# Two output products moved, eight scaled tiles given to ScalarE, and one softmax spread, in a state-space scan kernel

## The chip, the cores and the metric

The kernel runs on one core of a Trainium2 chip. The time is the device time of one launch in microseconds; the median of several runs is compared. Five engines work side by side, each through its own list of instructions in order, and hand work to each other with semaphores: TensorE (PE; its weight loads are listed as PEld), VectorE (DVE), ScalarE (ACT), GpSimd (POOL) and SyncE (SP), which issues the transfers.

## The reference, cut to what matters

One block on x of shape (2, 1024, 256): a row gate, a Mamba layer, then an attention and a gated network on its output. What the change touches is the Mamba recurrence and its projection, and the attention's scores:

```python
def step(h, inputs):
    d_t, x_t, B_t, C_t = inputs
    dA = jnp.exp(d_t[..., None] * A)
    h = dA * h + (d_t * x_t)[..., None] * B_t[:, None, :]
    y = jnp.einsum('bds,bs->bd', h, C_t)      # 16 states are summed
    return (h, y)
...
y = ys.transpose(1, 0, 2) + xi * D
y = y * jax.nn.silu(z)
return x + y @ out_proj                        # the output product
...
scores = jnp.einsum('bhte,bhse->bhts', qmod, k) / jnp.sqrt(jnp.asarray(e, x.dtype))
attn = jax.nn.softmax(scores, axis=-1)
```

There are 512 channels, 16 states to a channel, 1024 positions in each of two batches. All is computed in float32.

## The kernel before, in words

The positions are cut into four chunks of 512 (two to a batch). A chunk passes 16 states; a counter n from 0 to 63 runs over chunk and state, c = n // 16 and s = n % 16. For every n the work is:

- ACT makes four exponentials dA (L1259, one to each 128 channels), DVE runs four scans over the 512 positions (L1727), and POOL has written the scans' other input into a ring of four tiles beforehand (L1403).
- PE turns the four position tiles of the scanned state (`transposes`, L834) into the two banks of `hT`: tiles 0 and 2 into bank 0, tiles 1 and 3 into bank 1. They are turned in the order 1, 0, 3, 2. Tile 3 waits until tile 1 has been read from its bank, tile 2 until tile 0 has.
- Tiles 0 and 2 are scaled by C on ACT (L1269, `mul_step`) and added up by PE in `yacc` (`reduce`, L597, with the skip products of L593 in a chunk's first state). Tiles 1 and 3 are scaled and added into `yTd` by DVE (`mac_step`): L1747 for s > 0, and L1740 for s = 0, which starts the sum without adding. For some states tile 3 is scaled by ACT (L1278) and added by POOL (L1415).

Everything else is cut into jobs, each one product group of PE in one of two banks `pp` that take turns in the jobs' order (`INDEX`), and its reader or readers on ACT or DVE. Tables place them by hand in half states: a chunk has 32, two to a state, the even one being served before exp_step(n, 2) on ACT and before scan_step(n, 2) on DVE. A job at half state h is issued by PE in h, and read by ACT and DVE in h + 1. In an even half PE issues `transposes(n - 1, 1)` first, then the jobs, then tiles 0, 3 and 2. A job waits until the job two before it has been read. The tables are `PROLOGUE` (the next chunk's input: T the transposed input, I and Z the input products, V the convolutions, X, XT and D the products for B, C and delta), `EPILOGUE` (the chunk before: Y the last sums times the gate, O the output products at L626 with their sum into `xt` at L1553, R their transposes), `LAST_EPILOGUE` for the same in the last chunk, and `ATT` (batch 0's attention, beside the last chunk). D's reader is long: ACT takes |x| from the bank (L1108), then an exponential and a logarithm (L1128, L1130), then DVE adds them (L1538) and frees the bank. S0 and S1 are the two halves of the scores (L698). S1's reader is the softmax: DVE adds and reduces (L1572 to L1580), ACT takes one exponential of 1024 columns (L1158), and DVE waits for it.

After state 63 a tail of 68 us follows: the last chunk's epilogue, batch 1's attention and the gated network.

## Time and profile before

| | |
|---|---|
| median of 3 runs | 565.59 us (562.24 to 568.28) |
| the profiled execution's own time | 562.97 us |
| its span in the profile | 561.2 us |
| first scan starts, last scan ends | 44.5 us, 493.5 us |
| busy PE, DVE, ACT, POOL | 481.0, 461.2, 372.5, 387.2 us |

The span is shorter than the device time by what lies around it. The busy times are sums over stages with different limits; a row of the timeline gives an instruction's start, its duration, its engine, line and operation, and in brackets how long the engine idled before it and what released it. Instructions of the same form that follow each other are merged in one row (x2, x4). One float32 product is recorded as two instructions, so 16 PE rows are 8 products.

### The profile page before, as it was taken

How to read it: one execution, taken by the hardware profiler on the slowest of the kernel's cores; microseconds unless marked ns; L12 is line 12 of the kernel's file. 1: busy time of each engine (PE TensorE's matmuls, PEld its weight loads, DVE VectorE, ACT ScalarE, POOL GpSimd, SP SyncE). 2: the span in 40 equal slices, each digit the busy share in tenths (PEclk: the TensorE clock that was granted, in tenths of full speed). 3: DMA queues.
4: the chain of work that ended last, by engine and by line, in shares of the span. 5: the costliest groups of instructions: out<-in, count | busy, mean ns of one | idle time of the engine just before them, and what ended most of it. 6: DMA issues, size and time to landing. Idle time of an engine off the chain costs nothing.

```text
span 561.2 us, 7944 instructions
## 1 busy us (share of the span) xinstructions
PE 481.0 (86%) x2777; PEld 348.8 (62%) x2777; DVE 461.2 (82%) x531; ACT 372.5 (66%) x650; POOL 387.2 (69%) x235
## 2 busy tenths in 40 slices
PE   8968999868768999987689999986897968899992
PEld 6423765455557665745576657656796856888651
DVE  4779989979999889799997897899998989851522
ACT  3676777769966767898757678897568668721210
POOL 5039978767996877879968778599789969510001
PEclk9987999979989999899899999598998869799997
DMA  8330111111111001111010111111111590029004
GB/s 289 115 116 38 39 38 39 40 40 37 39 37 39 38 39 39 40 39 39 39 39 37 39 37 41 38 38 38 39 39 39 201 369 1 2 87 353 2 1 155
DMA packets 17919, 38.88 MB, mean 69 GB/s; under 512 B 1665, under 2 KB 10497, under 8 KB 17874
## 3 DMA queue, kind: packets, MB, share of 16 engines
q1 hardware_dynamic: 17874, 38.32, 19.8%
q8 instruction: 24, 0.39, 0.3%
q14 instruction: 21, 0.17, 0.1%
HBM read 36.08 MB, written 2.23 MB: 68 GB/s over the span
## 4 chain that ended last, share of the span: by engine, by line
PE 49%; DVE 27%; issue 11%; ACT 10%; POOL 2%; DVEq 0%; ACTq 0%; POOLq 0%
DVE scanmem L1727 16%; PE hT L834 11%; PE pp L563 6%; PE pp L539 6%; PE yacc L597 5%; DVE yTd L1747 5%; PE pp L626 4%; ACT dA L1259 2%; PE dA L799 2%; PE pp L575 2%; PE pp L589 2%; ACT hc L1269 1%; PE pp L770 1%; PE pp L649 1%; DVE yTd L1652 1%
## 5 line engine op out<-in xcount | busy, mean ns | idle before, releaser
L1403 POOL TENSOR_TENSOR scanmem<-par,scanmem 128x1024 f32<-128x1024 f32 x128 | 300.9, 2370 | 79.7 <-PE hT L834 60.3
L834 PE MATMUL hT<-con,scanmem 128*128 128x128 f32 x1024 | 167.4, 298 | 54.0 <-DVE yTd L1747 32.0
L1259 ACT ACTIVATE dA<-par,Aneg 128x512 f32<-128x512 f32 x256 | 171.7, 690 | 56.0 <-DVE scanmem L1727 54.5
L834 PEld LDWEIGHTS hT<-con,scanmem 128*128 128x128 f32 x1024 | 126.7, 152 | 108.2 <-issue 34.3
L1727 DVE TENSOR_TENSOR_SCAN scanmem<-dA,carry,scanmem 128x512 f32<-128x512 f32 x128 | 156.7, 1266 | 11.9 <-ACT dA L1259 11.7
L1727 DVE TENSOR_TENSOR_SCAN scanmem<-dA,scanmem 128x512 f32<-128x512 f32 x128 | 148.9, 1204 | 8.5 <-ACT dA L1259 7.8
L1269 ACT ACTIVATE hc<-hT,CTs 128x512 f32<-128x512 f32 x128 | 87.1, 680 | 43.5 <-PE hT L834 43.3
L597 PE MATMUL yacc<-con,hc 128*128 128x128 f32 x512 | 86.6, 297 | 0.3 <-ACT hc L1269 0.3
L597 PEld LDWEIGHTS yacc<-con,hc 128*128 128x128 f32 x512 | 69.4, 157 | 0.6 <-ACT hc L1269 0.6
L1747 DVE SCALAR_TENSOR_TENSOR yTd<-hT,CTs,yTd 128x512 f32<-128x512 f32 x85 | 62.0, 729 | 8.4 <-PE hT L834 7.5
L539 PE MATMUL pp<-xnT,wi 128*128 128x512 f32 x120 | 59.0, 620 | 3.4 <-ACT xnT L1038 2.1
L563 PE MATMUL pp<-xr,diag 128*128 128x512 f32 x112 | 50.2, 592 | 0.0
L1463 POOL TENSOR_TENSOR par<-xt,hc 128x1024 f32<-128x1024 f32 x1 | 2.4, 2350 | 53.0 <-ACT hc L1319 53.0
L539 PEld LDWEIGHTS pp<-xnT,wi 128*128 128x128 f32 x120 | 21.6, 198 | 22.2 <-issue 17.4
L563 PEld LDWEIGHTS pp<-xr,diag 128*128 128x128 f32 x112 | 20.3, 189 | 21.1 <-issue 20.9
L626 PE MATMUL pp<-wo,par 128*128 128x256 f32 x128 | 29.0, 381 | 0.5 <-DVE par L1507 0.5
L1415 POOL TENSOR_TENSOR yTd<-yTd,sm 128x512 f32<-128x512 f32 x21 | 26.9, 1280 | 0.0
L626 PEld LDWEIGHTS pp<-wo,par 128*128 128x128 f32 x128 | 23.8, 190 | 3.9 <-DVE par L1507 0.7
L1415 POOL TENSOR_TENSOR yTd<-yTd,xnT 128x512 f32<-128x512 f32 x14 | 17.8, 1274 | 8.1 <-ACT xnT L1278 8.1
L589 PE MATMUL pp<-dbc,wdt 17*128 17x512 f32 x28 | 17.3, 706 | 0.4 <-DVE xt L1553 0.3
L1538 DVE SCALAR_TENSOR_TENSOR par<-pp,par 128x512 f32<-128x512 f32 x14 | 9.6, 688 | 9.3 <-ACT par L1130 6.4
L799 PE MATMUL dA<-con 128*128 128x128 f32 x110 | 17.1, 289 | 0.0
(195 smaller groups left out, 510.8 us busy)
## 6 DMA issues: line engine op xcount, KB each, us to landing
scanmem<-brow SPq DMA_DIRECT2D x32, 512.0 KB, 3.6
par<-in SPq DMA_DIRECT2D x1, 4096.0 KB, 17.3
scanmem<-in SPq DMA_DIRECT2D x1, 4096.0 KB, 15.0
xt<-in SPq DMA_DIRECT2D x4, 512.0 KB, 6.7
wi<-in SPq DMA_DIRECT2D x2, 1024.0 KB, 6.7
out<-par SPq DMA_DIRECT2D x4, 512.0 KB, 4.1
aw<-in SPq DMA_DIRECT2D x5, 256.0 KB, 6.7
xr<-in SPq DMA_DIRECT2D x1, 1024.0 KB, 8.9
```

The source lines that it names most:

```text
L539: last = mm(o, win[:, k, col:col + P], xnT[:, k, :], start=k == 0, stop=k == KD - 1)
L563: last = mm(o, dg[:, m, k, :], xr3[:, m, k:k + T], start=k == 0, stop=k == KC - 1)
L589: return mm(o, wdt[:, m * P:(m + 1) * P], dbc[0:DR + 1, :], start=True, stop=True)
L597: return mm(o[:, m * P:(m + 1) * P], src, ident, start=False, stop=last, is_transpose=True, skip_group_check=True)
L626: last = mm(o[:, i * DM:(i + 1) * DM], dx(e)[:, m, t0:t0 + P], wo[:, m, :], start=m == 0, stop=m == CT - 1)
L834: last = nc.tensor.transpose(hT[:, i % 2, m * P:(m + 1) * P], hb[:, n % RING, m, i * P:(i + 1) * P], ident)
L1259: A(dA[:, m % 2, :], delta(c)[:, m, :], ACT.Exp, scale=Aneg[:, m * NS + s:m * NS + s + 1]).then_inc(da_ready, 1)
L1269: A(hc[:, e % 2, :], hT[:, 0, :], ACT.Copy, scale=CTs[:, c % 2, i, s:s + 1]).then_inc(mul_done, 1)
L1403: nc.gpsimd.tensor_tensor(hb[:, n % RING, ms, :], dx(c)[:, ms, :], Bb[:, row:row + 1, :].to_broadcast([P, 2, T]), ALU.mult).then_inc(bx_re ...
L1415: nc.gpsimd.tensor_tensor(dst, dst, for_pool(n), ALU.add).then_inc(pool_sum_done, 1)
L1727: V.tensor_tensor_scan(hb[:, n % RING, m, :], dA[:, m % 2, :], hb[:, n % RING, m, :], start, ALU.mult, ALU.add).then_inc(scan_done, 1)
L1747: V.scalar_tensor_tensor(dst, src, cs, dst, ALU.mult, ALU.add).then_inc(mac_done, 1)
```

## The change

1. In `EPILOGUE`, for chunks 0 and 1 (read beside chunks 1 and 2), output product ("O", 0) stands at half state 18 instead of 11 and ("O", 1) at 20 instead of 18.
2. The first state's tiles 1 and 3 of every chunk are written into `yTd` by ACT (`first_sum`) instead of by DVE: eight instructions of 128x512. A semaphore of their own, `first_sum_done`, replaces `mac_done` for those states, and `wait_sum` chooses between them. On ACT they stand in state 1 of the chunk: tile 1 after mul_step and carry_step, ahead of the jobs and of exp_step(n, 2); tile 3 after mul_step(n - 1, 0).
3. In `ATT`, S1 moves from half state 17 to 18, PT from 20 to 21, YV, YT and VV from 22, 23, 24 to 23, 24, 25, and WO from 27 to 28.

```diff
-EPILOGUE = {1: [("Y", 1), ("Y", 3)], 11: [("O", 0)], 18: [("O", 1)], 28: [("R", 0)], 30: [("R", 1)]}
+EPILOGUE = {1: [("Y", 1), ("Y", 3)], 18: [("O", 0)], 20: [("O", 1)], 28: [("R", 0)], 30: [("R", 1)]}
-ATT = [7, 8, 8, 10, 12, 14, 15, 16, 17, 20, 22, 23, 24, 27]
+ATT = [7, 8, 8, 10, 12, 14, 15, 16, 18, 21, 23, 24, 25, 28]
...
+def scalar_sums(n, i):
+
+    return 2 * (n // NS) + (i + 1) // 2
...
+        def wait_sum(eng, n, i):
+
+            if n % NS == 0:
+                eng.wait_ge(first_sum_done, scalar_sums(n, i))
+            elif i == 3 and by_pool(n):
+                eng.wait_ge(pool_sum_done, pool_sums(n))
+            else:
+                eng.wait_ge(mac_done, vector_sums(n, i))
...
+            def first_sum(n, i):
+
+                c = n // NS
+                act.wait_ge(hT_ready, turned(n, i))
+                if c >= 2 and i == 1:
+                    wait_full(act, ("Y", c - 2, 3))
+                A(yTd[:, c % 2, i // 2, :], hT[:, 1, :], ACT.Copy, scale=CTs[:, c % 2, i, 0:1]).then_inc(first_sum_done, 1)
...
+                    if s == 1:
+                        first_sum(n - 1, 1)
                     for job in to_read(2 * n):
                         read(job)
                     exp_step(n, 2)
...
                     if n:
                         mul_step(n - 1, 0)
                         pool_mul_step(n - 1)
+                    if s == 1:
+                        first_sum(n - 1, 3)
...
-                if i == 3 and by_pool(n):
+                if s == 0 or i == 3 and by_pool(n):
                     return
                 dve.wait_ge(hT_ready, turned(n, i))
                 dst = yTd[:, c % 2, i // 2, :]
                 src, cs = hT[:, 1, :], CTs[:, c % 2, i, s:s + 1]
-                if s == 0:
-                    if c >= 2 and i == 1:
-                        wait_full(dve, ("Y", c - 2, 3))
-                    V.tensor_scalar(dst, src, cs, None, ALU.mult).then_inc(mac_done, 1)
...
+                wait_sum(dve, n - 1, i)
+                V.scalar_tensor_tensor(dst, src, cs, dst, ALU.mult, ALU.add).then_inc(mac_done, 1)
```

How PE's list changes around half states 10 to 12 of chunk 1 (L563 is V, L626 is O; the transposes and sums are L834 and L597). Before:

```order
L563 MATMUL pp<-xr,diag 128x512 x4
L834 MATMUL hT<-con,scanmem 128x128 x8
L597 MATMUL yacc<-con,hc 128x128 x4
L834 MATMUL hT<-con,scanmem 128x128 x4
L597 MATMUL yacc<-con,hc 128x128 x4
L626 MATMUL pp<-wo,par 128x256 x8
L834 MATMUL hT<-con,scanmem 128x128 x4
L563 MATMUL pp<-xr,diag 128x512 x4
L834 MATMUL hT<-con,scanmem 128x128 x8
```

Now (all lines are 15 further down in the new file):

```order
L578 MATMUL pp<-xr,diag 128x512 x4
L849 MATMUL hT<-con,scanmem 128x128 x8
L612 MATMUL yacc<-con,hc 128x128 x4
L849 MATMUL hT<-con,scanmem 128x128 x4
L612 MATMUL yacc<-con,hc 128x128 x4
L849 MATMUL hT<-con,scanmem 128x128 x4
L578 MATMUL pp<-xr,diag 128x512 x4
L849 MATMUL hT<-con,scanmem 128x128 x8
```

The eight products O are gone from between one state's last sum and the next state's first transposes, and V follows those at once.

PE's list at half states 18 to 21 of chunk 1 (L598 is XT, L604 is D, L641 is O), in the new file:

```order
L641 MATMUL pp<-wo,par 128x256 x8
L849 MATMUL hT<-con,scanmem 128x128 x8
L612 MATMUL yacc<-con,hc 128x128 x4
L849 MATMUL hT<-con,scanmem 128x128 x4
L612 MATMUL yacc<-con,hc 128x128 x4
L598 MATMUL pp<-con,dbc 128x49 x4
L604 MATMUL pp<-dbc,wdt 128x512
L849 MATMUL hT<-con,scanmem 128x128 x4
L641 MATMUL pp<-wo,par 128x256 x8
L604 MATMUL pp<-dbc,wdt 128x512
L849 MATMUL hT<-con,scanmem 128x128 x8
```

Before, the same rows stood here without the second L641: the second D followed four transposes directly. Now O's eight products stand between them, and ahead of the transposes of tiles 0 and 3.

ACT's list in states 16 to 18, where chunk 1 begins (L1274 exponentials, L1284 the scaled tiles for PE, L1301 the new first sums, L1053 T's reader), in the new file:

```order
L1274 ACTIVATE dA<-par,Aneg 128x512 x2
L1284 ACTIVATE hc<-hT,CTs 128x512
L1301 ACTIVATE yTd<-hT,CTs 128x512
L1274 ACTIVATE dA<-par,Aneg 128x512 x2
L1284 ACTIVATE hc<-hT,CTs 128x512
L1301 ACTIVATE yTd<-hT,CTs 128x512
L1274 ACTIVATE dA<-par,Aneg 128x512 x2
L1284 ACTIVATE hc<-hT,CTs 128x512
L1053 ACTIVATE xnT<-pp,vec 128x512 x2
```

Before, the two L1301 were absent. The first now stands ahead of state 17's last two exponentials and of the scaling of tile 0.

## Rows read from the trace of the kernel before

**Rows 1.** The page: span, and the chain that ended last.

```profile
span 561.2 us, 7944 instructions
...
PE 49%; DVE 27%; issue 11%; ACT 10%; POOL 2%; DVEq 0%; ACTq 0%; POOLq 0%
```

**Rows 2.** Groups by line: busy us, mean ns, idle before, releasers.

```profile
L1740 DVE TENSOR_SCALAR yTd<-hT,CTs 128x512 f32<-128x512 f32 x8 | 5.8, 729 | 0.3 <-PE hT L834 0.2
```

**Rows 3.** Timeline, states 20 to 23: start, us, engine, line, operation.

```profile
202.65 3.62 PE L626 MATMUL pp<-wo,par 128*128 128x256 f32 x16
...
203.06 0.72 DVE L1747 SCALAR_TENSOR_TENSOR yTd<-hT,CTs,yTd 128x512 f32<-128x512 f32 x1
...
206.10 0.60 PE L834 MATMUL hT<-con,scanmem 128*128 128x128 f32 x4
...
206.54 3.60 PE L563 MATMUL pp<-xr,diag 128*128 128x512 f32 x8
...
210.62 0.69 ACT L1269 ACTIVATE hc<-hT,CTs 128x512 f32<-128x512 f32 x1 [3.74 <-PE hT L834]
...
213.15 2.45 DVE L1727 TENSOR_TENSOR_SCAN scanmem<-dA,carry,scanmem 128x512 f32<-128x512 f32 x2
```

**Rows 4.** Timeline of states 37 and 38, same place in chunk 2.

```profile
315.29 0.72 DVE L1747 SCALAR_TENSOR_TENSOR yTd<-hT,CTs,yTd 128x512 f32<-128x512 f32 x1
...
318.95 0.60 PE L834 MATMUL hT<-con,scanmem 128*128 128x128 f32 x4
```

**Rows 5.** Timeline of states 25 and 26, chunk 1.

```profile
234.57 1.12 PE L589 MATMUL pp<-dbc,wdt 17*128 17x512 f32 x2
...
235.63 1.95 PE L834 MATMUL hT<-con,scanmem 128*128 128x128 f32 x8
...
237.41 0.69 DVE L1538 SCALAR_TENSOR_TENSOR par<-pp,par 128x512 f32<-128x512 f32 x1 [1.51 <-ACT par L1130]
...
238.43 0.67 ACT L1269 ACTIVATE hc<-hT,CTs 128x512 f32<-128x512 f32 x1
```

**Rows 6.** Windows: us, busy (instructions) of PE, PEld, DVE, ACT, POOL, PEclk, DMA.

```profile
241.00:245.00 4.00, 2.75 (x13) 1.37 (x13) 4.00 (x6) 3.94 (x7) 3.57 (x2) 1.00 0.00 0
...
352.00:356.00 4.00, 4.00 (x12) 2.17 (x12) 3.97 (x5) 3.61 (x7) 3.29 (x2) 0.50 0.00 0
```

**Rows 7.** Timeline of states 17 and 18, where chunk 1 begins.

```profile
169.28 0.69 ACT L1259 ACTIVATE dA<-par,Aneg 128x512 f32<-128x512 f32 x1 [1.84 <-DVE scanmem L1727]
...
170.56 0.75 DVE L1740 TENSOR_SCALAR yTd<-hT,CTs 128x512 f32<-128x512 f32 x1
171.08 0.67 ACT L1269 ACTIVATE hc<-hT,CTs 128x512 f32<-128x512 f32 x1
...
172.30 0.60 PE L834 MATMUL hT<-con,scanmem 128*128 128x128 f32 x4
...
174.06 1.95 PE L533 MATMUL pp<-par,xt 128*128 128x128 f32 x16
...
176.10 1.26 ACT L1038 ACTIVATE xnT<-pp,vec 128x512 f32<-128x512 f32 x2
```

**Rows 8.** Timeline of states 49 and 50, where chunk 3 begins.

```profile
397.73 0.66 PE L834 MATMUL hT<-con,scanmem 128*128 128x128 f32 x4 [1.11 <-DVE yTd L1740]
...
402.02 3.69 PE L626 MATMUL pp<-wo,par 128*128 128x256 f32 x16
402.40 2.45 DVE L1727 TENSOR_TENSOR_SCAN scanmem<-dA,carry,scanmem 128x512 f32<-128x512 f32 x2
```

**Rows 9.** Timeline of states 56 and 57: batch 0's S1, R and softmax.

```profile
448.78 0.60 ACT L1141 ACTIVATE x1T<-pp 128x512 f32<-128x512 f32 x1 [1.02 <-PE pp L698]
...
449.86 0.68 DVE L1572 TENSOR_TENSOR sm<-pp,negm 128x512 f32<-128x512 f32 x1
...
452.68 1.15 ACT L1158 ACTIVATE sm<-sm,st 128x1024 f32<-128x1024 f32 x1 [3.29 <-DVE st L1580]
...
454.53 4.83 DVE L1727 TENSOR_TENSOR_SCAN scanmem<-dA,carry,scanmem 128x512 f32<-128x512 f32 x4 [0.41 <-ACT dA L1259]
```

More of the change, by code:

```diff
@@ L163, in pool_sums @@
     return sum(by_pool(j) for j in range(n + 1))
+def scalar_sums(n, i):
+    return 2 * (n // NS) + (i + 1) // 2
 def vector_sums(n, i):
-    return 2 * n + (i + 1) // 2 - pool_sums(n if i == 3 else n - 1)
+    return 2 * n + (i + 1) // 2 - pool_sums(n if i == 3 else n - 1) - 2 * (n // NS + 1)
 def to_read(h):
@@ L346, in build @@
         pool_mul_done, pool_sum_done = sem("pool_mul_done"), sem("pool_sum_done")
+        first_sum_done = sem("first_sum_done")
         carry_done, gated = sem("carry_done"), sem("gated")
@@ L826, in transposes @@
                 if i == 3:
-                    pe.wait_ge(mac_done, vector_sums(n, 1))
+                    wait_sum(pe, n, 1)
                 if i == 1 and n:
@@ L831, in transposes @@
                     else:
-                        pe.wait_ge(mac_done, vector_sums(n - 1, 3))
+                        wait_sum(pe, n - 1, 3)
                 for m in range(CT):
@@ L1408, in add_step @@
                 if by_pool(n):
-                    if by_pool(n - 1):
-                        pool.wait_ge(pool_sum_done, pool_sums(n - 1))
-                    else:
-                        pool.wait_ge(mac_done, vector_sums(n - 1, 3))
+                    wait_sum(pool, n - 1, 3)
                     pool.wait_ge(pool_mul_done, pool_sums(n))
@@ L1736, in mac_step @@
                 src, cs = hT[:, 1, :], CTs[:, c % 2, i, s:s + 1]
-                if s == 0:
-                    if c >= 2 and i == 1:
-                        wait_full(dve, ("Y", c - 2, 3))
-                    V.tensor_scalar(dst, src, cs, None, ALU.mult).then_inc(mac_done, 1)
-                else:
-                    if i == 3 and by_pool(n - 1):
-                        dve.wait_ge(pool_sum_done, pool_sums(n - 1))
-                    else:
-                        dve.wait_ge(mac_done, vector_sums(n - 1, i))
-                    V.scalar_tensor_tensor(dst, src, cs, dst, ALU.mult, ALU.add).then_inc(mac_done, 1)
+                wait_sum(dve, n - 1, i)
+                V.scalar_tensor_tensor(dst, src, cs, dst, ALU.mult, ALU.add).then_inc(mac_done, 1)
             for c in range(NCH):
```

## The prediction

> **What bounds the kernel now.** I read the page first, then the groups by line, then the timeline in those places that the change touches, and the windows for TensorE's clock. The page's chain of waits goes through PE for 49% and DVE for 27% of a span of 561.2 us [rows 1]: neither engine alone sets the pace, and a saving on one of them counts only in those states in which the chain runs through it. The tail behind the last scan is not touched. So the sum is made state by state: for each place, which wait ends last before the next state's first scan, and by how much that moves.
>
> **Part 1a, O leaves half state 11: a gain.** In chunk 1, ("O", 0) starts at 202.65 and takes 3.62 us [rows 3]. Behind it in PE's list stand state 21's transposes of tile 1 at 206.10 and then V at 206.54. What these transposes need is a sum of DVE that begins at 203.06 and takes 0.72, so they could have begun at 203.85. V's 3.60 us then stand ahead of the transposes of tile 0, for which ACT waits 3.74 us until 210.62, and behind ACT's copy stand V's two readers, two exponentials, and the scans of state 23 at 213.15 [rows 3]. The whole chain from 206.10 to 213.15 hangs on PE, so it moves forward by 206.10 - 203.85 = 2.25 us. The next candidate is DVE itself: it loses O's two sums between the scans of state 22 and gets tile 1 earlier, so it is through before V's reader can run, and does not cut the gain. In chunk 2 the same sum of DVE begins at 315.29, and the transposes stand at 318.95 instead of about 316.1 [rows 4]: 2.85 us. Together **-5.1 us**. Nothing of O's work has vanished; it stands elsewhere.
>
> **Part 1b, an O at half state 18.** There ("O", 1) stood, now ("O", 0) stands: eight products and two sums of DVE for the same. Zero.
>
> **Part 1c, O enters half state 20: a loss.** The second product D starts at 234.57, and the next transposes at 235.63 [rows 5]. Now O stands ahead of D: from about 234.5, 3.62 us [rows 3] to 238.1. D itself must now wait for the first D's bank, since O took the turn between them; DVE reads that bank from 237.41 for 0.69, to 238.10 [rows 5], just covered by O. D starts at 238.2, the transposes of tile 0 at 238.2 + 1.06 = 239.25, done at about 239.85. ACT took them at 238.43 [rows 5]. ACT is the bound here, with the table load, softplus and exponentials; so 3.6 us of O meet 2.2 us of room, and its list moves back by 239.85 - 238.43 = 1.4 us. Behind that copy are the second D's readers and state 27's exponentials, all of which move with it. O's two sums on DVE fit in DVE's wait for the second softplus. Twice (chunks 1 and 2): **+2.8 us**, if PE keeps its full clock.
>
> It may not. PE took 1.95 us for eight transposes at 235.63 [rows 5] where four follow each other in 0.44 at full clock (206.10 to 206.54 [rows 3]), so about 1.1 for eight: the low level, 1.2 GHz, had just set in after the light work of XT and D. The price has these ends. If all of O runs at the low level in both chunks, it takes 3.6 us more each time, +7.2. Or the denser work of O ends the low stretch sooner: in chunk 2, at 352 to 356, PE shows a granted clock of 0.50 and is busy 4.00 us for 12 instructions, where the like stretch of chunk 1, at 241 to 245, shows 1.00 and 2.75 us for 13 [rows 6]; taking that away is worth up to 1.25 us there. I take zero between them: one effect offsets the other, and the rows are nearest to a stretch that begins at full clock. "TensorE: Matmul & The Clock Gate" in the Trainium skill, Part 1 (the warmup mystery), says that the clock gate gives full rate to a busy array and half rate after idling. By that rule O is good for the clock once it runs, but starts behind light work; the sum would be anywhere between the two ends.
>
> **Part 2, the first sums go to ACT.** Eight instructions of 0.729 us leave DVE, 5.8 us in all [rows 2], and eight enter ACT's list. Copies of this shape take ACT 0.67 [rows 7]. What counts is what is queued behind them. In chunk 1 the exponential of state 17 ran at 169.28, while tile 1 was ready to be read only just before 170.56 [rows 7]. Now ACT waits for tile 1, copies it from 170.4 on, and does both exponentials behind it, so that the scaling of tile 0 moves from 171.08 to 172.4. DVE, freed of two instructions, would reach state 18 1.1 us sooner. But the transposes of tile 2 need that scaled tile's bank: PE, which came there at 172.30 [rows 7], starts at 173.1, and T moves from 174.06 to 174.9 and ends at 176.8. Its last copy ends at 177.5, where it ended before at 176.10 + 1.26 = 177.4 [rows 7]. The input products and the exponentials of state 19 hang on that copy. DVE's gain is gone two states later: 0 in chunk 1, and the same order gives 0 in chunk 2. In chunk 0 the copy stands ahead of Z's two readers on ACT and delays them and T by some 0.3 to 0.6 us, against 0.85 us that DVE gains: 0 again. Each of these zeros could be 0.5 off either way.
>
> Chunk 3 has no T behind it. There PE's transposes of tile 3 wait 1.11 us for DVE's first sum until 397.73 [rows 8]; ACT can now copy tile 1 before its exponentials are due. DVE drops two instructions, about 1.3 us with their overlap; ACT's second copy gives 0.2 of it back ahead of state 50's exponential. The last gate, O at 402.02 and state 50's scans at 402.40 [rows 8] come 1.1 us sooner. Nothing there restores the old time: **-1.1 us**.
>
> **Part 3, S1 one half state later.** PE now issues S1 after state 56's transposes of tile 1, so 0.44 us later (the step of four in [rows 3]). R's reader on ACT must wait for S1, since it overwrites what S1 reads: it ran at 448.78, after a wait of 1.02 [rows 9], and now runs at 449.2, and state 57's last two exponentials follow it. DVE's second pair of scans starts at 450.4 instead of 454.53 [rows 9], but the softmax now stands behind them: from 449.86 (DVE) by 452.68 (ACT) to 454.53 (next scans) it took 4.7 us [rows 9], and it takes them again, since state 58's exponentials are queued behind the softmax's exponential. State 58 would start at 457.5; it started at 454.53 + 2.4 = 456.9 [rows 9]. In exchange, the copies for PE and POOL are made ahead of the stall instead of behind it, and state 58 loses its own wait: about 0.9 us back. Together **-0.3 us**; ends are -1.5 and +2, the latter if nothing is given back and R waits longer. PT to WO one half state later are small products in states with room: zero.
>
> **Sum:** -5.1 + 2.8 - 1.1 - 0.3 = **-3.7 us**. The profiled execution took 562.97 us, which gives 559.3. The median of the runs is 565.59, 2.6 us above that execution, so the number that I give is 565.6 - 3.7 = **561.9 us**. The runs of before lie within 6 us of each other, and about 1% (5.7 us) is what can be told from no change.
>
> **Rivals.** *DVE is the bound (chance 0.27).* Then the first sums' gain of 1.1 us is kept in all four chunks: three times 1.1 = 3.3 us more, -7.0, 558.6; with the clock's 1.25 of chunk 2, 557.4. For it: DVE shows no idle time ahead of its first sum in state 17 [rows 7], and T's copy ends only 0.1 us late by my walk. Against: state 19 is released by ACT and PE. "Perfetto Trace Analysis" in the Trainium skill, section Optimizing Scalar/DVE Operations, says that offloading from a saturated DVE to Scalar may make sense; by that rule the 5.8 us would count in full, a sum of -8.4. No row has DVE saturated over the whole stage.
>
> *O at half state 20 runs at the low clock (0.15); the one that ends slower.* PE's activity before it is XT, D and four transposes, and behind these it had fallen to half rate at 235.6 [rows 5]. With all of O low in both chunks, +7.2: the sum is +3.5, 569.1 us. It turns from a gain to a loss once the two O lose more than 3.7 us together, that is when more than half of them runs at 1.2 GHz.
>
> *The softmax round trip gets worse (0.16).* R's reader waits for S1, and DVE's stall is paid in full with nothing given back: +2 in place of -0.3, -1.4, 564.2.
>
> *Nothing much done:* the order shows that the instructions do move, so this is no case of its own.
>
> My forecast has the remaining 0.42. Its own range, with 0.5 for each zero and the runs' spread, is 558.5 to 565. For 8 in 10 the range must take in the DVE case and the softmax case and most of the run-to-run spread: **555.5 to 567.5**. Faster by over 1% (under 559.9): 0.24 from the DVE case and 0.11 from the lower part of mine, 0.35. Slower by over 1% (above 571.2): a third of the low-clock case and a bad draw of runs, 0.10. Within 1%: 0.55.
>
> **What would show it.** State 22, which ended at 213.15 and read ("O", 0) before, should be 2 us shorter, and its V should start within 1 us of the end of DVE's sum; so in chunk 2. State 26 should be 1.4 us longer, with ACT waiting on PE for tile 0 behind O and D. State 17 should be about 1 us shorter and states 18 and 19 take it back; chunk 3's state 49 should be shorter for good. The softmax should stand after state 57's fourth scan, with DVE still idle until ACT is through. Wrong would be: O's 16 instructions taking over 5 us, gaps on ACT in state 17 that reach the scans, or state 19 starting earlier by the full 1.1 us.

## The result: slower by half a per cent

| | before | after |
|---|---|---|
| median beside each other, 20 runs each | 562.44 us | 564.09 us |
| lowest and highest run | 558.79, 568.57 us | 561.0, 568.74 us |
| profiled execution's own time | 562.97 us | 566.36 us |
| span in the profile | 561.2 us | 564.6 us |
| mean granted clock of TensorE in it | 0.929 | 0.923 |

The ratio of after to before is 1.0054, with a 95% interval of 1.0028 to 1.0080: 3.0 us slower (1.6 to 4.5), where the prediction had 3.7 us faster. The ratio leaves out a kernel's runs that are over 1.5% above its fastest, which are five of the kernel before at 568 us and none of the new one, so the two medians over all runs are only 1.7 us apart, and the size of the rise is less sure than the interval says. Its 561.9 us were set against a first median of 565.59; beside the 20 runs the same sum gives 558.7. The rise is inside "within 1%", which had the largest chance, but the sign is wrong, and the reasons for the sign are what follows.

The page of the kernel after, beside [rows 1]; parts left out:

```profile
span 564.6 us, 7944 instructions
...
PE 51%; DVE 25%; issue 10%; ACT 9%; POOL 3%; DVEq 0%; ACTq 0%; POOLq 0%
```

DVE's share of the chain fell by 2 points, PE's rose by 2 and POOL's by 1. The L1740 group of [rows 2] is gone; eight rows of ACT, L1301, do its work. A time per state shows where the sum came apart. A state's length runs from the start of its first scan to that of the next state's; the table has those that changed by over 0.8 us.

| states | after - before, us | predicted |
|---|---|---|
| 22 and 38 (O left half state 11) | -2.3, -2.8 | -2.25, -2.85 |
| 26 and 42 (O came into 20) | +1.5, +1.5 | +1.4, +1.4 |
| 43 | -1.5 | up to -1.25, left out of the sum |
| 1, 2 (first sums, chunk 0) | -1.0, +2.7 | sum zero |
| 18 (chunk 1) | +1.4 | sum zero |
| 32, 33, 34 (chunk 2) | -0.9, -1.6, +1.1 | sum zero |
| 49 (chunk 3) | -1.3 | -1.1 |
| 57, 58 (softmax) | +3.7, -1.3 | +0.6, -0.9 |
| 11, 44, 55, 59 | +0.9, +0.9, -1.2, +1.0 | nothing |

States 10 to 12 together are 1.9 longer, though no instruction of them was moved; the kernel with part 3 alone has the like there.

One profiled execution stands here against one, and much of what the table shows comes and goes without any edit. State 43 is 8.8 us long before; it is 7.3 us in e3, e5, e7 and e16 too, which leave the outputs where they were. State 55 is 1.2 us shorter in every other profile of this case. State 58 is 6.9 us before and 5.6 us after; it is 5.5 to 5.7 us in e9, e10, e13 and e15 too, which leave S1 where it was. The tail behind the last scan, where nothing was edited, takes 67.7 us before, 69.2 us after, and 72.3 us in e10, with a granted clock of 0.94, 0.94 and 0.87. So a difference is put down to an edit below only where it comes with the edit in the other profiles too.

**Part 1 came out as worked out.** Timeline of PE and ACT in states 21 and 22, after, which answers to [rows 3]; columns are start, us, engine, line, operation, and in brackets idle time and releaser:

```profile
209.07 0.63 PE L849 MATMUL hT<-con,scanmem 128*128 128x128 f32 x4 [0.75 <-DVE yTd L1762]
209.54 3.60 PE L578 MATMUL pp<-xr,diag 128*128 128x512 f32 x8
...
213.62 0.69 ACT L1284 ACTIVATE hc<-hT,CTs 128x512 f32<-128x512 f32 x1 [1.43 <-PE hT L849]
```

PE now waits for DVE's sum, 0.75 us, and V follows the transposes at once. ACT waits 1.43 us for V's end, not 3.74. Timeline of PE in state 26, after, beside [rows 5]:

```profile
237.48 3.62 PE L641 MATMUL pp<-wo,par 128*128 128x256 f32 x16
241.15 1.12 PE L604 MATMUL pp<-dbc,wdt 17*128 17x512 f32 x2
242.20 1.09 PE L849 MATMUL hT<-con,scanmem 128*128 128x128 f32 x8
```

O runs at the full clock (3.62 us, as in [rows 3]), so the rival in which it runs at the low one is out. All seven other profiles that have O in half state 20 show states 22, 26, 38 and 42 changed by the same amounts, within 0.2 us.

**Part 3 did not.** DVE and POOL in state 57, after, beside [rows 9]:

```profile
451.01 0.69 DVE L1600 TENSOR_REDUCE st<-sm 128x1 f32<-128x512 f32 x1
451.74 4.69 DVE L1602 TENSOR_TENSOR st<-st 128x1 f32<-128x1 f32 x1
456.46 0.15 DVE L1604 TENSOR_SCALAR st<-st 128x1 f32<-128x1 f32 x1
...
458.50 2.46 DVE L1751 TENSOR_TENSOR_SCAN scanmem<-dA,carry,scanmem 128x512 f32<-128x512 f32 x2 [0.41 <-ACT dA L1274]
```

```profile
448.23 4.66 POOL L1430 TENSOR_TENSOR scanmem<-par,scanmem 128x1024 f32<-128x1024 f32 x2
452.85 1.25 POOL L1439 TENSOR_TENSOR yTd<-yTd,xnT 128x512 f32<-128x512 f32 x1
454.07 2.33 POOL L1430 TENSOR_TENSOR scanmem<-par,scanmem 128x1024 f32<-128x1024 f32 x1
```

The larger of two numbers per partition takes DVE 4.69 us. It ends at 456.43, and POOL, which had no gap since 448.23, ends its last instruction at 456.40. The same instruction in the kernel before, a row that the prediction did not read, with POOL beside it, whose last instruction ended at 452.44:

```profile
451.29 1.16 DVE L1578 TENSOR_TENSOR st<-st 128x1 f32<-128x1 f32 x1
```

```profile
450.09 2.35 POOL L1403 TENSOR_TENSOR scanmem<-par,scanmem 128x1024 f32<-128x1024 f32 x1
```

**Nor did part 2 in chunk 0.** ACT and PE in states 0 and 1, after:

```profile
54.34 0.69 ACT L1301 ACTIVATE yTd<-hT,CTs 128x512 f32<-128x512 f32 x1 [3.22 <-PE hT L849]
54.92 1.07 ACT L1117 ACTIVATE par<-pp 128x512 f32<-128x512 f32 x2
55.87 1.31 ACT L1274 ACTIVATE dA<-par,Aneg 128x512 f32<-128x512 f32 x2
57.10 0.69 ACT L1284 ACTIVATE hc<-hT,CTs 128x512 f32<-128x512 f32 x1
```

```profile
57.84 1.11 PE L849 MATMUL hT<-con,scanmem 128*128 128x128 f32 x4 [2.12 <-ACT hc L1284]
58.75 1.91 PE L608 MATMUL yacc<-par,diagD 128*128 128x128 f32 x8
```

The same stretch before:

```profile
52.36 0.60 ACT L1102 ACTIVATE par<-pp 128x512 f32<-128x512 f32 x1 [1.06 <-PE pp L539]
54.07 0.60 ACT L1102 ACTIVATE par<-pp 128x512 f32<-128x512 f32 x1 [1.12 <-PE pp L539]
54.57 0.69 ACT L1259 ACTIVATE dA<-par,Aneg 128x512 f32<-128x512 f32 x1
...
56.26 0.67 ACT L1269 ACTIVATE hc<-hT,CTs 128x512 f32<-128x512 f32 x1
```

ACT idles 3.22 us at the first sum. Two readers of Z's bank and two exponentials, which ran at 52.36 to 56.3 before, stand behind it. PE then idles 2.12 us for tile 0. When it starts again its products take 1.91 us, where eight of this form take 1.06 at full clock: the low level, 1.2 GHz (the granted clock is 0.50 from 58 to 61 us). States 0 to 4 are together 1.9 us longer.

Chunks 1 and 2 show no loss of this kind. State 18 is 1.4 us longer in five of the six profiles that have both sums of chunk 1 on ACT (2.6 in e13), but state 17 is up to 1.6 us shorter; the five states from 16 on are together between 1.3 us shorter and 1.1 us longer, and without these sums they are between 1.0 us shorter and 0.9 us longer. In chunk 2 the spread is as wide: 1.3 shorter to 1.7 longer with the sums, 1.1 shorter to 1.3 longer without.

### The profile page after: what moved, and what is told of

It reads as the page before. It is cut to its first block, busy times and chain, and to the rows that moved or that the text cites. A ratio compares the mean times of both kernels' runs of the same rounds, so it can differ in the third digit from the quotient of the medians.

```text
span 564.6 us, 7944 instructions
## 1 busy us (share of the span) xinstructions
PE 482.8 (86%) x2777; PEld 347.8 (62%) x2777; DVE 460.1 (81%) x523; ACT 376.6 (67%) x658; POOL 386.6 (68%) x235
## 4 chain that ended last, share of the span: by engine, by line
PE 51%; DVE 25%; issue 10%; ACT 9%; POOL 3%; DVEq 0%; ACTq 0%; POOLq 0%
DVE scanmem L1751 14%; PE hT L849 12%; PE pp L578 6%; PE pp L554 6%; PE yacc L612 5%; DVE yTd L1762 4%; PE pp L641 3%; PE pp L604 2%; PE dA L814 2%; POOL scanmem L1430 2%; ACT dA L1274 2%; PE pp L590 2%; PE pp L713 1%; PE yacc L608 1%; PE pp L664 1%
## 5 line engine op out<-in xcount | busy, mean ns | idle before, releaser
L849 PE MATMUL hT<-con,scanmem 128*128 128x128 f32 x1024 | 164.8, 295 | 56.9 <-DVE yTd L1762 33.0
L1274 ACT ACTIVATE dA<-par,Aneg 128x512 f32<-128x512 f32 x256 | 171.3, 690 | 40.2 <-DVE scanmem L1751 38.7
L849 PEld LDWEIGHTS hT<-con,scanmem 128*128 128x128 f32 x1024 | 124.2, 151 | 112.1 <-issue 34.1
L1284 ACT ACTIVATE hc<-hT,CTs 128x512 f32<-128x512 f32 x128 | 87.0, 680 | 42.7 <-PE hT L849 42.6
L612 PEld LDWEIGHTS yacc<-con,hc 128*128 128x128 f32 x512 | 67.9, 155 | 0.6 <-ACT hc L1284 0.6
L554 PE MATMUL pp<-xnT,wi 128*128 128x512 f32 x120 | 60.4, 632 | 2.3 <-DVE par L1554 1.4
L641 PE MATMUL pp<-wo,par 128*128 128x256 f32 x128 | 29.0, 381 | 0.5 <-DVE par L1531 0.5
L641 PEld LDWEIGHTS pp<-wo,par 128*128 128x128 f32 x128 | 23.8, 190 | 3.8 <-DVE par L1531 0.7
L604 PE MATMUL pp<-dbc,wdt 17*128 17x512 f32 x28 | 17.3, 706 | 0.9 <-DVE xt L1577 0.7
```

What stands on the lines that cost most here:

```text
L554: last = mm(o, win[:, k, col:col + P], xnT[:, k, :], start=k == 0, stop=k == KD - 1)
L612: return mm(o[:, m * P:(m + 1) * P], src, ident, start=False, stop=last, is_transpose=True, skip_group_check=True)
L641: last = mm(o[:, i * DM:(i + 1) * DM], dx(e)[:, m, t0:t0 + P], wo[:, m, :], start=m == 0, stop=m == CT - 1)
L849: last = nc.tensor.transpose(hT[:, i % 2, m * P:(m + 1) * P], hb[:, n % RING, m, i * P:(i + 1) * P], ident)
L1274: A(dA[:, m % 2, :], delta(c)[:, m, :], ACT.Exp, scale=Aneg[:, m * NS + s:m * NS + s + 1]).then_inc(da_ready, 1)
L1284: A(hc[:, e % 2, :], hT[:, 0, :], ACT.Copy, scale=CTs[:, c % 2, i, s:s + 1]).then_inc(mul_done, 1)
```

## The experiments

All ratios are to the kernel before, run beside on the same chip, with 95% intervals; two experiments may have run on different chips. A ratio is not the quotient of the two medians: for e10 the medians give 1.005 and for e12 0.990, where the ratios are 1.0011 and 0.9863. Lengths of states are from one profiled execution each, against that of the kernel before. The expectations of e13, e15, e16 and e17 speak of eight chunks and that of e14 of the last chunk of each batch; the kernel has four chunks, with two first sums each, and e14 has those of chunk 3 alone.

### One part at a time

**e1: the outputs alone** (part 1).

```diff
-EPILOGUE = {1: [("Y", 1), ("Y", 3)], 11: [("O", 0)], 18: [("O", 1)], 28: [("R", 0)], 30: [("R", 1)]}
+EPILOGUE = {1: [("Y", 1), ("Y", 3)], 18: [("O", 0)], 20: [("O", 1)], 28: [("R", 0)], 30: [("R", 1)]}
```

> The kernel before with only the two output products moved (half states 18 and 20 instead of 11 and 18). Theory (the output move is a gain, the loss is elsewhere): states 22 and 38 shorter by 2.3 and 2.8 us, states 26 and 42 longer by 1.5 each, so -2 us, or -3.5 if state 43 keeps its full clock; ratio to the kernel before 0.994 to 0.997. Rival (the output move itself loses, because the products now stand in front of the softplus readers): ratio above 1.000, with states 26 and 42 longer by 3 us or more each.

Measured 559.18 us, ratio 0.9955 (0.9924 to 0.9986), 2.5 us faster; the sum had 2.3. States 22 -2.1, 26 +1.5, 38 -2.7, 42 +1.5.

**e2: the first sums alone** (the change without its `EPILOGUE` and `ATT`).

> The kernel before with only the eight first sums given to ScalarE. Theory (ScalarE's list holds the scaled tile 0 and so T back; light work makes TensorE fall to 1.2 GHz there): chunk 0 slower by 1.5 us or more over states 1 to 3, chunk 1 slower by 0 to 1.5 over states 17 to 19, chunk 2 0 to -2, chunk 3 -1.3; ratio 0.999 to 1.004. Rival (VectorE is the bound, its 5.8 us are saved): ratio 0.990 to 0.994, states 1, 17, 33 and 49 shorter by 1.1 with nothing given back.

Measured 566.0 us, ratio 1.0080 (1.0042 to 1.0118): 4.5 us slower, where the sum had 1.1 faster. State 49 is 1.3 shorter, as worked out; states 1 and 2 together are 1.5 longer. The mean granted clock over its runs is 0.913, against 0.928 over those of the kernel before beside it. The expectation (0.999 to 1.004) missed the size as well.

**e3: the scores apart alone.**

```diff
-ATT = [7, 8, 8, 10, 12, 14, 15, 16, 17, 20, 22, 23, 24, 27]
+ATT = [7, 8, 8, 10, 12, 14, 15, 16, 18, 21, 23, 24, 25, 28]
```

> The kernel before with only the attention table of the change (S1 one half state later, PT to WO too). Theory (the softmax's maximum of 128x1, a VectorE instruction with both operands in SBUF, waits until GpSimd pauses, and now meets three of its instructions in a row): that instruction takes over 3 us instead of 1.16, state 57 is longer by 3 us or more, ratio 1.003 to 1.007. Rival (it is only the copy that waits for S1 and the exponentials behind the softmax, as I forecast): the maximum stays near 1.2 us, states 57 to 59 together within 1 us of before, ratio 0.998 to 1.002.

Measured 562.75 us, ratio 1.0036 (1.0010 to 1.0063): 2.0 us slower, state 57 longer by 3.5, 58 shorter by 1.3. DVE in state 57, and POOL beside it:

```profile
455.21 4.51 DVE L1578 TENSOR_TENSOR st<-st 128x1 f32<-128x1 f32 x1
```

```profile
451.52 4.67 POOL L1403 TENSOR_TENSOR scanmem<-par,scanmem 128x1024 f32<-128x1024 f32 x2
456.13 1.28 POOL L1415 TENSOR_TENSOR yTd<-yTd,xnT 128x512 f32<-128x512 f32 x1
457.35 2.35 POOL L1403 TENSOR_TENSOR scanmem<-par,scanmem 128x1024 f32<-128x1024 f32 x1
```

It ends at 459.72 and POOL at 459.70. The 1.3 us of state 58 are not shown to come from the move, as said above. The three parts make -0.45 + 0.80 + 0.36 = +0.7%; together they were +0.54%.

### The small instruction that waits for GpSimd

The theory: this operation of DVE, with two inputs in SBUF, cannot run while POOL reads there. Its edit writes the second half's maximum beside the score's and takes the larger with a reduction of one input.

```diff
-                own.mark(V.reduce_max(st[:, 0:1], sm[:, 512:1024], AX.X))
+                own.mark(V.reduce_max(st[:, 3:4], sm[:, 512:1024], AX.X))
...
-                own.mark(V.tensor_tensor(st[:, 0:1], st[:, 0:1], st[:, 4:5], ALU.max))
+                own.mark(V.reduce_max(st[:, 0:1], st[:, 3:5], AX.X))
```

**e4: the whole change with this edit.**

> The changed kernel with one instruction in another form: the maximum of the two halves' maxima is a reduction over two adjacent columns instead of an operation on two SBUF operands; the result is the same. Theory (waiting for GpSimd is the loss of the third part): the instruction takes under 0.3 us instead of 4.69, state 57 falls from 13.8 to 9.3 us, the ratio to the kernel before falls from 1.005 to about 0.997. Rival (something else holds VectorE there, such as the semaphore of the reduction before it, or ScalarE's list): the instruction or the one behind it takes as long as before, state 57 stays above 12 us.

Measured 558.66 us, ratio 0.9945 (0.9913 to 0.9976), against 1.0054 without the edit. DVE in state 57, and POOL beside it:

```profile
449.84 0.15 DVE L1602 TENSOR_REDUCE st<-st 128x1 f32<-128x2 f32 x1
...
452.07 2.46 DVE L1751 TENSOR_TENSOR_SCAN scanmem<-dA,carry,scanmem 128x512 f32<-128x512 f32 x2 [0.41 <-ACT dA L1274]
```

```profile
446.33 4.68 POOL L1430 TENSOR_TENSOR scanmem<-par,scanmem 128x1024 f32<-128x1024 f32 x2
450.97 1.27 POOL L1439 TENSOR_TENSOR yTd<-yTd,xnT 128x512 f32<-128x512 f32 x1
452.19 2.35 POOL L1430 TENSOR_TENSOR scanmem<-par,scanmem 128x1024 f32<-128x1024 f32 x1
```

POOL is as busy as in the kernel after, and the same maximum takes 0.15 us. State 57 is 0.8 shorter than before the change, not 3.7 longer. This turns the sign of the whole. The gain is larger than expected (0.997): 6.1 us between the two ratios, where state 57 lost 4.5. State 2, the same code in both, is 1.6 us shorter in e4's profile, at full clock where the kernel after had the low one, so the rest need not come from the edit.

**e5: the edit on the kernel before**, and **e6: the edit with part 1.**

> The kernel before with only the softmax's maximum in the reduction form. In the kernel before this instruction took 1.16 us in batch 0 and 0.16 in batch 1. Theory (the wait for GpSimd depends on where the softmax meets its list): at the old place there is only 1.0 us to win, ratio 0.997 to 0.999, against 6 us at the new place. Rival (the form of the instruction is faster in itself, whatever the place): a gain like that at the new place, ratio below 0.993.

> The output products moved and the reduction form, nothing else of the change. Theory (the parts add up): 0.9955 times 0.998, so 0.993 to 0.995; it is then as fast as or faster than the changed kernel with the reduction form (0.9945), since the first sums cost and the later S1 with the reduction form gains. Rival (the first sums do help beside the moved outputs): 0.998, slower than 0.9945 by 2 us or more.

e5 560.64 us, 0.9987 (0.9949 to 1.0024): before the change the maximum took 1.16 us, so there was little to win; state 57 is 1.0 shorter. e6 560.57 us, 0.9969 (0.9932 to 1.0006), which cannot be told from e1, and lies between its theory (0.993 to 0.995) and its rival (0.998). The edit is worth most where the wait is long, and it was S1's new place that made it long (e3): the maximum now falls into a row of POOL's work. That row is longer too. ACT's copy for POOL, which ran at 455.62 behind the softmax's exponential before, now runs at 449.02 ahead of it, and POOL takes it up at 452.85.

### Which of the first sums lose, and why

A list `FIRST_SUMS` of (chunk, tile) says which go to ACT; the others stay on DVE.

**e7: chunks 0 to 2, both tiles; e8: chunk 3 alone, with parts 1 and 3 and the reduction.**

```diff
+FIRST_SUMS = [(0, 1), (0, 3), (1, 1), (1, 3), (2, 1), (2, 3)]
...
+FIRST_SUMS = [(3, 1), (3, 3)]
```

> The kernel before with first sums on ScalarE in chunks 0, 1 and 2 only, not in chunk 3. Theory (ScalarE's copy holds up T in the three chunks that have a T, and helps only in chunk 3): ratio above that of all eight by the 1.1 to 1.3 us of chunk 3, so 1.008 to 1.012, state 49 as before. Rival (all chunks alike, or the loss is only a scatter of the clock): ratio near 1.004 or 1.000.

> The output products moved, S1 and the jobs behind it later as in the change, the reduction form, and first sums on ScalarE in chunk 3 alone. Theory (each part kept where it gains): outputs 0.9955, later S1 without its wait about -1 to -2 us, chunk 3's first sums -1.2 us: 0.988 to 0.991, the fastest so far; it beats the all-eight version (0.9945) by the 2 to 5 us that the first sums cost in chunks 0 to 2. Rival (the first sums in chunks 0 to 2 cost nothing): 0.9945 again.

e7 566.86 us, 1.0062 (1.0013 to 1.0110): slower, though not above e2, as expected (1.008 to 1.012) if chunk 3 gains. e8 556.19 us, 0.9915 (0.9872 to 0.9957), the lowest median of all, but its interval overlaps that of e4 (0.9945), so these times do not show by themselves what chunks 0 to 2 cost. What shows chunk 3's gain is state 49: 1.3 us shorter in each of the nine profiles that have both its sums on ACT, 0.7 with one of them, and unchanged with none.

**e9: tile 3 alone, all chunks; e10: chunk 0 alone, both tiles**, on the kernel before.

```diff
+FIRST_SUMS = [(0, 3), (1, 3), (2, 3), (3, 3)]
...
+FIRST_SUMS = [(0, 1), (0, 3)]
```

> The kernel before with first sums on ScalarE for tile 3 alone, in all four chunks; tile 1 stays with VectorE. Theory (the cost comes from tile 1's copy, for which ScalarE waits with two exponentials and tile 0's scaling behind it): states 2 and 18 within 0.5 us of before, ratio 0.998 to 1.001. Rival (any copy more on ScalarE at the start of a chunk costs): half of the loss of all eight, ratio 1.004.

> The kernel before with first sums on ScalarE in chunk 0 alone. Theory (here the copy also holds up the readers of the gate's products, and TensorE idles 2 us for tile 0): state 1 shorter by 1.0, state 2 longer by 1.1 at full clock or 2.5 at the low one, so 0 to +1.5 us, ratio 1.000 to 1.003. Rival (chunk 0 holds the whole loss of all eight): 1.006 or more.

e9 563.56 us, 1.0000 (0.9967 to 1.0033). e10 565.6 us, 1.0011 (0.9979 to 1.0044), states 1 -1.0 and 2 +1.1. Neither tile 3 nor chunk 0 alone shows a cost, but the intervals leave room for 1.9 and 2.5 us.

**e15: tile 1 alone, all chunks** (`FIRST_SUMS` of tile 1).

> On the kernel before, only the first sum of tile 1 goes to ScalarE, in all eight chunks; with tile 3 alone the ratio was 1.000. Theory: tile 1's sum stands ahead of the scaled tile that the next products wait for, so it carries most of the loss; ratio 1.003 to 1.008, and state 2 of the trace is 1 us or more longer. Rival: neither tile alone loses anything and only both together do; 0.999 to 1.002.

568.72 us from six runs, 1.0105 (1.0059 to 1.0152), above the 1.003 to 1.008 expected: no smaller a loss than e2's, with half of the instructions. Not all of it lies at the sums. The profiled execution is 7.6 us longer than that of the kernel before; 4.5 us of this is the tail, at a granted clock of 0.87 for 0.94, and 1.9 us is chunk 0 (states 0 to 4). ACT and PE in chunk 0:

```profile
54.88 0.69 ACT L1309 ACTIVATE yTd<-hT,CTs 128x512 f32<-128x512 f32 x1 [3.22 <-PE hT L857]
...
57.65 0.69 ACT L1292 ACTIVATE hc<-hT,CTs 128x512 f32<-128x512 f32 x1
```

```profile
58.40 0.65 PE L857 MATMUL hT<-con,scanmem 128*128 128x128 f32 x4 [2.12 <-ACT hc L1292]
58.89 1.86 PE L616 MATMUL yacc<-par,diagD 128*128 128x128 f32 x8
```

and ACT in the same place with tile 3 alone (e9), where all runs in its old order:

```profile
53.26 0.60 ACT L1125 ACTIVATE par<-pp 128x512 f32<-128x512 f32 x1 [1.12 <-PE pp L562]
...
55.43 0.67 ACT L1292 ACTIVATE hc<-hT,CTs 128x512 f32<-128x512 f32 x1
56.16 0.69 ACT L1309 ACTIVATE yTd<-hT,CTs 128x512 f32<-128x512 f32 x1
```

**e13: the first sums of e2, with PE kept busy.** Twelve products more, into a sum not yet in use, at each chunk's first scan state.

```diff
+                    if s == 1:
+                        if c:
+                            pe.wait_ge(gated, 2 * (c - 1) + 1)
+                        keep_warm(12, yacc[:, 0, 0:P])
```

> The first scaled tiles of all eight chunks go to the sums on ScalarE, nothing else of the change, and TensorE gets twelve additional products into a sum that is not yet in use, in the stretch at each chunk's first scan state in which it waited 2.1 us for ScalarE's scaled tile 0. Theory clock: what this part loses (ratio 1.008 so far, granted clock 0.911 in its profiled execution) is TensorE being slowed after that idle stretch; with the stretch filled the mean granted clock is above 0.925 and the ratio 0.997 to 1.003. Rival, ScalarE's queue: the added work on ScalarE delays what TensorE and VectorE wait for, whatever TensorE does meanwhile; the ratio stays 1.005 to 1.010.

566.94 us, 1.0096 (1.0063 to 1.0129). The mean granted clock of its runs is 0.928, that of e2's 0.913, and the low stretch behind 57 us is gone; the time is not better. In chunk 0, where PE stood idle, it helps: states 0 to 4 are 0.6 us longer than before the change, against 1.7 in e2. Elsewhere the products took 2.84 us where the gap in chunk 1 was 0.70 (e2), so they delay the transposes behind them, and in chunk 3 state 50 is 2.0 us longer:

```profile
172.50 2.84 PE L814 MATMUL yacc<-con 128*128 128x128 f32 x24
175.18 0.60 PE L849 MATMUL hT<-con,scanmem 128*128 128x128 f32 x4
```

It shows that the clock alone, bought in this way, does not bring the loss back, not how large the clock's part is.

**e16: e15 with the sum behind the exponentials in ACT's order.**

```diff
-                    if s == 1 and by_scalar(n - 1, 1):
-                        first_sum(n - 1, 1)
                     for job in to_read(2 * n):
                         read(job)
                     exp_step(n, 2)
                     exp_step(n, 3)
+                    if s == 1 and by_scalar(n - 1, 1):
+                        first_sum(n - 1, 1)
```

> As the run with tile 1's first sum alone on ScalarE in all eight chunks (ratio 1.0105), except that in ScalarE's order the sum stands behind the parameter evictions of that half state and behind the factors 2 and 3 of the next state, and no longer ahead of them. In that run ScalarE stood 3.22 us idle at 54.88 us for the transposes before the sum, with two parameter evictions and two factors behind it that could have run. Theory, the place in ScalarE's order: the ratio falls to between 0.999 and 1.004 and ScalarE's first scaled tile of chunk 0 comes within 0.7 us of where it was before. Rival, the added 0.7 us of ScalarE work itself or TensorE's wait for another engine: the ratio stays at 1.007 or above.

564.97 us, 1.0039 (1.0007 to 1.0072): 0.66 of the 1.05% is the place by the middle values, though the two intervals overlap and the runs are from two chips. In the profiles it is 0.5 us of chunk 0: states 0 to 4 are 1.4 us longer than before, against 1.9 in e15. What is left there is seen in its trace, ACT and PE in chunk 0:

```profile
54.33 0.60 ACT L1125 ACTIVATE par<-pp 128x512 f32<-128x512 f32 x1 [1.12 <-PE pp L562]
...
56.50 0.67 ACT L1309 ACTIVATE yTd<-hT,CTs 128x512 f32<-128x512 f32 x1
57.07 0.68 ACT L1292 ACTIVATE hc<-hT,CTs 128x512 f32<-128x512 f32 x1
```

```profile
57.23 1.24 PE L857 MATMUL hT<-con,scanmem 128*128 128x128 f32 x8 [2.06 <-ACT yTd L1309]
```

The evictions are no longer behind the sum (the second at 54.33, against 54.07 before), but now PE waits 2.06 us for the sum itself, and still falls to the low clock at 58.3.

**e17: all parts in all chunks, with the reduction and this order.**

> All parts of the change in all eight chunks, the softmax's maximum as a reduction (as in the run with all but the port wait, 0.9945), and tile 1's first sum behind the evictions and factors in ScalarE's order. If the place in the order was the whole loss, this is at or below the best version: ratio 0.985 to 0.991. If the first sums of chunks 0 to 2 are worth nothing or lose wherever they stand, it is 0.992 to 0.996, above the version that has them in the last chunk alone (0.9915).

557.99 us, 0.9944 (0.9910 to 0.9978), the same as e4's 0.9945. In the whole change the order of tile 1 brings nothing that can be measured.

### Around the best version

**e11: the second output at half state 24, not 20; e12: S1 at its old place; e14: PE kept busy in the softmax** (24 products at state 58's half, in ScalarE's stall), each on e8.

```diff
-EPILOGUE = {1: [("Y", 1), ("Y", 3)], 18: [("O", 0)], 20: [("O", 1)], 28: [("R", 0)], 30: [("R", 1)]}
+EPILOGUE = {1: [("Y", 1), ("Y", 3)], 18: [("O", 0)], 24: [("O", 1)], 28: [("R", 0)], 30: [("R", 1)]}
...
-ATT = [7, 8, 8, 10, 12, 14, 15, 16, 18, 21, 23, 24, 25, 28]
+ATT = [7, 8, 8, 10, 12, 14, 15, 16, 17, 20, 22, 23, 24, 27]
...
+                    if n == 58:
+                        wait_free(("PT", 0, 0))
+                        keep_warm(24, bank(("PT", 0, 0))[:, 0:P])
```

> The best version so far (outputs moved, S1 later, reduction form, first sums in chunk 3 alone) with (O, 1) at half state 24 instead of 20. Theory (the 1.5 us of states 26 and 42 are O standing in front of the second D and of tile 0's transposes while ScalarE is full of softplus): both states shorter by 1.5 us; at 24 PE and ScalarE are less full and it costs under 1 us each: ratio 0.5% below that of half state 20. Rival (eight products cost about 1.5 us wherever they stand in an even half state): the ratio stays, state 28 or 29 longer by 1.5.

> The best version so far with S1 and the jobs behind it at their old half states. Theory (once the maximum no longer waits for GpSimd, the later place gains, because state 58 no longer waits and the scaled tiles are made ahead of the stall): state 58 longer by 1.3 us than in the version with S1 later, state 57 the same within 0.5, ratio 0.2 to 0.3% higher. Rival (the place of S1 is worth nothing by itself): ratio equal within 0.1%.

> The best version so far (outputs in half states 18 and 20, scores apart, maximum as a reduction, first sums on ScalarE in the last chunk of each batch only) with 24 additional products at state 57, where TensorE waits 4.1 us for ScalarE and is at the low clock from 448.6 to 455.4 us. Theory clock: states 57 to 59 are run at full clock and are 0.5 to 1.5 us shorter, ratio to the best version 0.997 to 0.999. Rival: these states are set by ScalarE and VectorE, which the clock doesn't touch; nothing changes within 0.3 us.

e11 560.34 us, 0.9967 (0.9941 to 0.9993), where 0.5% less than e8's 0.9915 was expected. States 26 and 42 are 1.5 shorter each than in e8, and 28 and 44 3.1 and 2.4 longer: half state 24 is the worse place. e12 557.15 us from six runs, 0.9863 (0.9813 to 0.9912): S1's place is worth nothing that can be told, once the wait for POOL is out; state 58 is 0.4 us longer than in e8, not the 1.3 expected. e14 557.68 us, 0.9900 (0.9865 to 0.9934), no different from e8. Windows of e8 and of e14 over the stall (us, busy and instructions of PE, PEld, DVE, ACT, POOL, then the granted clock):

```profile
450.00:455.00 5.00, 3.79 (x17) 3.39 (x18) 4.86 (x6) 4.24 (x8) 1.63 (x1) 0.50 1.02 422
```

```profile
450.00:455.00 5.00, 5.00 (x46) 5.00 (x46) 3.21 (x6) 4.10 (x7) 5.00 (x3) 1.00 1.04 405
```

The clock is full with the products, 0.50 without, and states 57 to 59 are together 0.3 us shorter, as the rival had it. The products took 5.62 us for a gap of 4.07, though, so some of what the clock gave was spent on them.

Three versions (e8, e12, e14) stand at 0.99 and beat both kernels. All have O at 18 and 20, the maximum as a reduction, and the first sums on ACT in chunk 3 alone.

## Why the prediction was wrong

**Part 1a and 1c: right.** -5.1 and +2.8 worked out, -5.1 and +3.0 in the states, -2.5 us in the run with this part alone against -2.3. The clock's 1.25 us of chunk 2, which I kept as an end, is not shown: state 43 is 1.5 shorter, but so it is in e3, e5, e7 and e16, without the outputs' move.

**Part 3: a step that failed, with its cause shown.** I took for the softmax "4.7 us ..., and it takes them again". That length was read from three rows, 449.86, 452.68 and 454.53 [rows 9], as if it were made of work and of waits within DVE and ACT. It held 1.16 us for a 128x1 maximum, which takes 0.15 us as a reduction (e4's row) and 0.16 us in its old form in batch 1, when POOL is idle; the surplus was a wait for POOL, whose length depends on what POOL is doing then. Moved, it became 4.69. The measured cost of the part is +2.0 us against -0.3 (e3). I had +2 as an end and 0.16 for "The softmax round trip gets worse"; the size was right, and that is luck, since the mechanism (R's reader waits) was not: that reader waited 1.46 us in the kernel after in place of 1.02, the 0.44 us of the forecast, and DVE idled about 0.1 us behind its sum before state 57's second pair of scans. That the wait for POOL is the cause is shown by e4, where POOL's rows have the same form and order and only the form of one instruction differs. The recovery that I had as 0.9 is not shown: state 58 is 1.3 shorter, and about as short in four profiles without the move.

**Part 2: chunk 3 right, chunk 0 not zero.** State 49 lost 1.3 us, against 1.1. For each of the others the prediction said 0, with 0.5 either way. Alone the part cost 4.5 us (e2), and 3.5 us without chunk 3 (e7). Two steps failed. For chunk 0 I had the sum "ahead of Z's two readers on ACT" and priced that at 0.3 to 0.6 us. I did not read that ACT would stand 3.22 us for the transposes; the scaled tile 0 comes 0.84 us later (57.10 against 56.26), and state 2 gets 2.7 longer. And I counted the delay of PE at full clock, though PE idles 2.12 us for that tile in chunk 0 and can run its next products at 1.2 GHz. It does not always do so. The same place in e4, whose code is the same up to state 56:

```profile
57.51 0.65 PE L849 MATMUL hT<-con,scanmem 128*128 128x128 f32 x4 [2.12 <-ACT hc L1284]
58.01 1.06 PE L608 MATMUL yacc<-par,diagD 128*128 128x128 f32 x8
```

Here, and in e10, PE stays at full clock behind the same gap (2.12 and 2.11 us), and states 0 to 4 cost 0.2 us, inside my 0.5. At the low clock (after, e2, e7) they cost 1.7 to 1.9. So in chunk 0 the order costs 0.2 us and the low clock about 1.6 more.

In chunks 1 and 2 my zero is not refuted: what states 17 and 33 gain, states 18 and 34 take back, within the spread. ACT waits there as well, in the kernel after in chunk 1:

```profile
175.84 0.69 ACT L1301 ACTIVATE yTd<-hT,CTs 128x512 f32<-128x512 f32 x1 [4.40 <-PE hT L849]
176.43 1.29 ACT L1274 ACTIVATE dA<-par,Aneg 128x512 f32<-128x512 f32 x2
```

State 17's last two exponentials, which ran at 169.28 and 170.46 in the old order, now wait with the sum for PE, whose Y products, ahead of those transposes, ran at the low clock (167 to 173.8). That tile 1 on ACT loses and tile 3 does not is shown by the times (e15 against e9: 1.0105 and 1.0000, intervals apart); that it is the place in the order is argued, from e16's 1.0039 and the rows of chunk 0.

**Which of the two turned the sign.** By the single parts it is part 2: -2.5 + 4.5 is a loss without part 3, and -2.5 + 2.0 is no loss without part 2. By e4 it is part 3: with its wait removed the whole gains, with part 2 in it. The parts do not add up. In the profiled execution the stretch from the first scan to the last is 2.1 us longer; without the 4.5 us that the maximum took above 0.15 it would be 2.5 shorter, and without chunk 0's 1.9 still 0.2 longer.

**Open** is where the rest of e2's 4.5 us lies, and why the sums' loss depends on the rest: it is 0.8% on the kernel before, but the whole change with the reduction (e4, 0.9945) is no slower than e6 (0.9969), which has none of the sums. The mean granted clock was 0.913 over e2's runs, 0.934 over those of e4 and of e6. By the slope at the end of this text, 0.015 less of clock goes with about 3.5 us, an estimate that would cover most of the 4.5; it is a correlation and not a cause. What decides in which stretches a version is granted the full clock was not found, and e13's and e14's products lengthened PE's list, so they do not isolate it.

**The rivals.** DVE as the bound is refuted: 5.8 us left DVE and the kernel lost (e2). "Perfetto Trace Analysis" in the Trainium skill, section Optimizing Scalar/DVE Operations, has it that such offloading may make sense from a saturated DVE; here it made sense in chunk 3 only. The one change of sign that I allowed for was a slow O, and it did not occur; a wait at R would have left a gain of 1.4 us.

## What to carry to other kernels

Before a step is moved, read every row of it, the 128x1 ones too: a duration well above that of its like can be a wait inside the instruction, and its price changes with the place. On an engine with an in-order list, an instruction that goes to it should stand where its input is already there; ask what is queued behind it while it waits, not only how long it runs. Where three edits come together, run them apart: one of them carried the gain, two took it back, and a fourth edit, of two lines, undid one of the two losses; on the kernel before it was worth nothing that could be told (e5). And before a state's change of a microsecond is put down to an edit, look at the same state in profiles without the edit.

## What the runs showed of the hardware

**A small instruction of DVE can wait through several instructions of POOL.** The 128x1 maximum of two inputs took 4.69 us (after) and 4.51 us (e3), past two boundaries between POOL's instructions, and ended within 0.03 us of the end of the third, behind which POOL was idle. As a reduction of one input it took 0.15 us beside the same work (e4). "SBUF — State Buffer" in the Trainium skill, sections SBUF: two separate sides and Who interferes with whom, names an exclusive lock on a port pair that such a `tensor_tensor` takes against POOL's reads, and says that `tensor_reduce` never contends. The rows agree with both; that DVE did not get its turn between two of POOL's instructions stands in these rows alone.

It is no matter of two inputs alone, and DVE does not always miss its turn. The kernel before has two TENSOR_SCALAR of 128x8, DVE and then POOL:

```profile
110.56 1.97 DVE L1656 TENSOR_SCALAR keep<-cnt,fr 128x8 f32<-128x8 f32 x1
112.56 1.19 DVE L1658 TENSOR_SCALAR keep<-keep 128x8 f32<-128x8 f32 x1
```

```profile
110.15 2.35 POOL L1403 TENSOR_TENSOR scanmem<-par,scanmem 128x1024 f32<-128x1024 f32 x1 [2.94 <-PE hT L834]
112.45 1.26 POOL L1415 TENSOR_TENSOR yTd<-yTd,sm 128x512 f32<-128x512 f32 x1
```

The first ends at 112.53 and POOL's instruction at 112.50; the second ends at 113.75, and POOL's at 113.71. The same two lines on 128x4, where POOL was idle, took 0.23 and 0.17 us. By these ends each waited for one instruction of POOL and got through there, though POOL's next followed at once. What makes the difference to the maximum was not found.

**The runs of one kernel scatter with the clock that they are granted.** Over the 138 runs of the kernel before that stood beside the experiments, 558.4 to 568.6 us, the time falls by 2.4 us for each 0.01 of mean granted clock (0.905 to 0.944), with a correlation of -0.82. The low clock stretched one place by 1.6 us in one execution and not in another of the same code up to there (chunk 0, after and e4). So a median from few runs, such as the 565.59 of three on which my number was set, can be 3 us off, about the size of every effect here.
